# First attention layer: the values' products of a pair of heads in two shared banks, and other steps for keys, values and weights

## The reference

```python
q = q * cos + _rotate_half(q) * sin
k = k * cos + _rotate_half(k) * sin
scores = jnp.einsum('bkgqd,bksd->bkgqs', qg, k) / jnp.sqrt(...)
scores = jnp.where(causal, scores, -jnp.inf)
attn = jax.nn.softmax(scores, axis=-1)
out = jnp.einsum('bkgqs,bksd->bkgqd', attn, v)
return jnp.einsum('bso,ho->bsh', out, Wo)
```

## Time and profile before

| | |
|---|---|
| median of 3 runs | 2199.09 us (2194.62 to 2199.65) |
| profiled execution | 2196.31 us, of which the span from first to last instruction is 2194.5 us |
| the first attention layer | about 34 to 760 us of the span |
| TensorE busy | 95% of the span |
| VectorE, ScalarE, GpSimd busy | 76%, 61%, 55% |

### The profile page before, as it was taken

How to read it: one execution, slowest core, us unless ns; L and a number is a source line. 1 busy time by engine, 2 the same in 40 slices (tenths; PEclk the granted TensorE clock), 3 DMA queues, 4 the chain that set the end, 5 groups by cost and what they waited for, 6 DMA issues and landing times. The chain is left out here.

```text
span 2194.5 us, 37916 instructions
## 1 busy us (share of the span) xinstructions
PE 2089.6 (95%) x10535; PEld 1756.7 (80%) x10535; DVE 1678.1 (76%) x2972; ACT 1349.4 (61%) x3637; POOL 1216.8 (55%) x985
## 2 busy tenths in 40 slices
PE   6999999999999778999999999999999999878998
PEld 4788888888888657888888888888888888756786
DVE  6788888888888876878888788888878888875422
ACT  5877777777776455656666565666656565544321
POOL 3878777787786554546454554545445463354300
PEclk9999999999999989999999999999999999979999
DMA  2534344434344422444444444434444343533210
GB/s 83 136 100 126 108 110 113 114 105 125 104 117 130 134 62 71 116 108 116 116 109 99 121 107 115 109 100 117 114 112 112 99 116 92 131 104 105 87 53 25
DMA packets 165887, 231.69 MB, mean 106 GB/s; under 512 B 47280, under 2 KB 77136, under 8 KB 165744
## 3 DMA queue, kind: packets, MB, share of 16 engines
q1 hardware_dynamic: 165744, 229.97, 39.4%
HBM read 114.23 MB, written 6.55 MB: 55 GB/s over the span
## 5 line engine op out<-in xcount | busy, mean ns | idle before, releaser
L90 POOL TENSOR_TENSOR l_probsT_lo<-l_moved,l_probsT_hi 128x512 fp32r<-128x512 f32 (+2 forms) x256 | 278.1, 1091 | 291.9 <-ACT l_probsT_hi L946 264.5
L940 ACT ACTIVATE l_probs<-l_score,l_negtop 128x512 f32<-128x512 f32 x256 | 176.1, 688 | 354.3 <-DVE l_negtop L1051 342.3
L90 DVE TENSOR_TENSOR l_probsT_lo<-l_moved,l_probsT_hi 128x512 fp32r<-128x512 f32 (+1 forms) x256 | 285.9, 1117 | 33.4 <-ACT l_probsT_hi L946 33.4
L1831 ACT ACTIVATE l_probs<-l_score,l_negtop 128x128 f32<-128x128 f32 (+3 forms) x256 | 135.0, 527 | 170.4 <-DVE l_negtop L1944 169.6
L1051 DVE TENSOR_REDUCE l_negtop<-l_score 128x1 f32<-128x512 f32 x256 | 175.5, 686 | 74.9 <-PE l_score L85 72.6
L83 PE MATMUL l_score<-l_kT_lo,l_qT_hi 128*128 128x512 f32 (+3 forms) x512 | 190.4, 372 | 24.1 <-POOL l_qT_lo L90 9.4
L83 PE MATMUL l_out<-l_w_out_lo,l_oT_hi 128*128 128x512 f32 x512 | 209.2, 409 | 2.8 <-DVE l_oT_lo L90 2.6
L84 PE MATMUL l_out<-l_w_out_hi,l_oT_lo 128*128 128x512 f32 x512 | 201.8, 394 | 0.0
L85 PE MATMUL l_out<-l_w_out_hi,l_oT_hi 128*128 128x512 f32 x512 | 201.5, 394 | 0.0
L83 PE MATMUL l_general<-l_w_qk_lo,xT_hi 128*128 128x512 f32 x504 | 198.1, 393 | 2.5 <-PEq L1451 2.5
L1944 DVE CUSTOM_DVE_ANT_0 l_score<-l_score,l_mask 128x128 f32<-128x128 f32 (+3 forms) x256 | 126.1, 493 | 96.9 <-PE l_score L85 95.5
(11 more groups left out here) (249 smaller groups left out, 6283.4 us busy)
## 6 DMA issues: line engine op xcount, KB each, us to landing
l_moved<-l_blocks SPq DMA_DIRECT2D x1024, 64.0 KB, 2.0
l_moved<-l_blocks SPq DMA_DIRECT2D x512, 80.0 KB, 2.1
l_inv_all<-inv_rows SPq DMA_DIRECT2D x32, 512.0 KB, 4.2
l_raw_out<-l_wo SPq DMA_DIRECT2D x64, 256.0 KB, 4.2
l_inv_all<-inv_rows SPq DMA_DIRECT2D x64, 256.0 KB, 3.6
l_raw_q<-l_wq SPq DMA_DIRECT2D x32, 256.0 KB, 4.1
l_raw_qk<-l_wq SPq DMA_DIRECT2D x64, 128.0 KB, 2.9
l_raw_qk<-l_wk SPq DMA_DIRECT2D x64, 128.0 KB, 3.0
```

What stands on the lines that cost most here:

```text
L90: return engine.tensor_tensor(out, full, hi.bitcast(F32), ALU.subtract)
L940: act.activation(probs[:, n % NPR], score[n % 2][:], ACT.Exp, bias=negtop[:, n:n + 1], accum_out=total[:, n:n + 1]).then_inc(s_exp, 1)
L1831: act.activation(probs[:, n % NPR, 0:width[t]], score[n % 2][:, 0:width[t]], ACT.Exp, bias=negtop[:, n:n + 1], scale=-1.0, accum_out=total ...
```

## The change

Values' products. The two slots of a pair share their banks by tokens, no longer one bank per head. The even slot of a pair now stands for tokens of tiles 0 and 1 of both heads (2 products: 512 columns for key chunk 0, 256 for chunk 1), the odd one for tiles 2 and 3 of both heads (4 products: 512, 256, 512, 512 columns for chunks 0, 3, 1, 2). The columns multiplied are the same, 2560 a pair, in 6 products instead of 8. The odd one stands a step later (4s + 22) and is cut in two halves. `cells` gives each transposed block its place, so that a product reads runs of equal cells, and `out_item` sets which head and tile a projection step takes.

Landing. `probsT` is landed by pair in 5 pieces of 512 instead of 8 pieces of 512, 384, 256 and 128, and all of it at steps 18 to 20 of the pair, where it stood at 16, 17, 20 and 21. VectorE still makes three pieces, GpSimd two.

Other steps. Keys stand at 16b - 10 (before -14), values at 16b + 14 (before 10), their transposition at 16b + 17 (before 14); the weights' steps are set one by one. The reading of `scaled` and `oT` for the odd slot follows its `pv`. `move` waits for TensorE's `pv` before the 16 DMAs, and for VectorE's reading of `inv_all` only before the one that overwrites it.

```diff
-MOVE0_AT, LAND0_AT, PV0_AT, OUT0_AT = 8, 16, 21, 26
-USES0 = {("q", s): 4 * s - 8 for s in range(SLOTS)} | {("pv", s): 4 * s + PV0_AT for s in range(SLOTS)}
-USES0 |= {(kind, b): 16 * b + n for kind, n in (("k", -14), ("v", 10), ("vt", 14)) for b in range(B)}
+MOVE0_AT, PV0_AT, OUT0_AT = 8, 21, 26
+LAND0_AT = {18: (0, 1), 19: (2, 3), 20: (4,)}
+PIECES0, EVEN0, ODD0 = 5, (0, 1, 4), (2, 3)
+USES0 = {("q", s): 4 * s - 8 for s in range(SLOTS)} | {("pv", s): 4 * s + PV0_AT + s % 2 for s in range(SLOTS)}
+USES0 |= {(kind, b): 16 * b + n for kind, n in (("k", -10), ("v", 14), ("vt", 17)) for b in range(B)}
...
-LOADS0 = {("wq", h): 4 * h - 13 for h in range(GH)} | {("wo", h): 4 * h + 22 for h in range(GH)}
-LOADS0 |= {("wk", 0): -19, ("wv", 0): 0}
+LOADS0 = {("wq", h): n for h, n in enumerate((-17, -12, -4, 0))} | {("wo", h): n for h, n in enumerate((23, 25, 31, 33))}
+LOADS0 |= {("wk", 0): -20, ("wv", 0): 4}
...
+        PV = ([(0, slice(12, 19, 2), slice(0, 4)), (1, slice(17, 20, 2), slice(2, 4))],
+              [(0, slice(0, 4), slice(0, 4)), (3, slice(13, 16, 2), slice(1, 4, 2)), (1, slice(4, 8), slice(0, 4)),
+               (2, slice(8, 12), slice(0, 4))])
+        def out_item(slot, n):
+            return (n % 2, n // 2, n % 2 * 2 + n // 2) if slot % 2 == 0 else (2 + n % 2, n // 2, n)
...
-            for lag, pieces in ((LAND0_AT, (0, 1)), (LAND0_AT + 1, (2, 3))):
+            for lag, pieces in LAND0_AT.items():
                 slot = m.slot_at(n, lag)
-                if slot is not None:
+                if slot is not None and slot % 2 == 0:
                     for e in pieces:
-                        yield slot, e
+                        yield slot // 2, e
...
-                    for k in range(TB):
-                        right = Split(chunk_columns(probsT_hi, slot, k),
-                                      chunk_columns(probsT_lo[:, slot // 2 % 2], slot, k))
-                        last = product(nc, by_block(bank[:])[:, :, k * 32:P].rearrange("p g (t i) -> p g t i", i=32),
-                                       v[:, j // GH, k * HD:(k + 1) * HD], right, k == 0, k == TB - 1)
+                    for k, at, to in [PV[1][c] for c in part] if odd else PV[0]:
+                        right = Split(probsT_hi[:, :, at], probsT_lo[:, pair % 2, :, at])
+                        last = product(nc, bank[:].rearrange("p (g e i) -> p g e i", g=TB, e=TB)[:, :, to],
+                                       v[:, j // GH, k * HD:(k + 1) * HD], right, k == 0, k == (1, 2)[odd])
...
             def halves(x):
-                return x[0] in ("q", "k", "v")
+                return x[0] in ("q", "k", "v") or x[0] == "pv" and x[1] % 2
...
-                    slot = m.slot_at(n, PV0_AT + 3)
-                    if slot is not None:
-                        output_lo(m, slot)
+                    for odd in range(2):
+                        slot = m.slot_at(n - odd, PV0_AT + 3)
+                        if slot is not None and slot % 2 == odd:
+                            output_lo(m, slot)
```

More of the change, by code:

```diff
@@ L1610, in move @@
                     was = 2 * pair - 3
-                    sp.wait_ge(s_free, m.done(USES0, ("pv", was % SLOTS), was // SLOTS, of_dve))
+                    sp.wait_ge(s_bank, m.done(USES0, ("pv", was % SLOTS), was // SLOTS))
                     sp.nop(nofuse=True)
@@ L1617, in move @@
                 wait_past(sp, s_inv_dma, m, 32 * (SLOTS // 2), 32 * pair + 16)
+                if not (m.first and pair < 2):
+                    sp.nop(nofuse=True)
+                    sp.wait_ge(s_free, m.done(USES0, ("pv", was % SLOTS), was // SLOTS, of_dve))
                 sp.dma_start(inv_all[:, k], inv_rows[k].rearrange("p t -> (p t)").unsqueeze(0).to_broadcast([P, P * PAIR]))\
@@ L1668, in bank_use @@
                 if kind == "pv":
-                    if m.last and d == 0 and j == SLOTS - 1:
+                    if m.last and d == 0 and j == SLOTS - 1 and 0 in part:
                         linear.brief_taken(pe)
@@ L1749, in body @@
                         project(m, x, d)
-                    for x, d in m.turns(USES0, n + 1) if n + 1 < TILES else []:
+                    for x, d in m.turns(USES0, n + 1) if n + 1 < TILES or m.last else []:
                         if halves(x):
@@ L1831, in exponentials, with landed_hi @@
                 act.activation(probs[:, n % NPR, 0:width[t]], score[n % 2][:, 0:width[t]], ACT.Exp,
-                               bias=negtop[:, n:n + 1], scale=-1.0, accum_out=total[:, n:n + 1]).then_inc(s_exp, 1)
-            def landed_hi(m, slot, e):
-                pair = slot // 2
-                if slot % 2 == 0 and e == 0:
+                               bias=negtop[:, n:n + 1], scale=-1.0, accum_out=total[:, column(n):column(n) + 1]).then_inc(s_exp, 1)
+            def landed_hi(m, pair, e, n):
+                if e == 0 and n >= TILES or e == 2:
+                    if not (m.first and pair == 0):
+                        was = 2 * pair - 1
+                        act.wait_ge(s_bank, m.done(USES0, ("pv", was % SLOTS), was // SLOTS))
+                        act.nop(nofuse=True)
+                if e == 0:
                     wait_past(act, s_move[pair % 2], m, SLOTS // 4 * MOVES, (pair // 2 + 1) * MOVES)
-                act.activation(chunk_row(probsT_hi, slot, e), chunk_row(moved[:, pair % 2], slot, e), ACT.Copy)\
-                    .then_inc(s_land_hi, 1)
+                act.activation(piece(probsT_hi, e), piece(moved[:, pair % 2], e), ACT.Copy).then_inc(s_land_hi, 1)
             def output_hi(m, x, d):
@@ L1866, in body @@
                             output_hi(m, x, d)
-                    for slot, e in landing(m, n):
-                        landed_hi(m, slot, e)
+                    for pair, e in landing(m, n):
+                        landed_hi(m, pair, e, n)
                     for x, d in m.turns(USES0, n, 5):
@@ L1961, in turn_blocks, with landed_lo @@
                 rows = blocks[:, pair % 2]
-                to = rows[:, :, 0:t + 1, t + 1] if slot % 2 == 0 else rows[:, :, t, 0:t + 1]
-                dve.transpose(to.rearrange("p c k i -> p k c i"), probs[:, n % NPR, 0:width[t]]).then_inc(s_block, 1)
-            def landed_lo(m, slot, e):
-                wait_past(dve, s_land_hi, m, TILES, TB * slot + e + 1)
-                k = slot // 2 % 2
-                rest(dve, chunk_row(probsT_lo[:, k], slot, e), chunk_row(moved[:, k], slot, e),
-                     chunk_row(probsT_hi, slot, e)).then_inc(s_lo_even, 1)
+                dve.transpose(rows[:, :, cells(slot, t)].rearrange("p c k i -> p k c i"), probs[:, n % NPR, 0:width[t]]).then_inc(s_block, 1)
+            def landed_lo(m, pair, e):
+                wait_past(dve, s_land_hi, m, PIECES0 * SLOTS // 2, PIECES0 * pair + e + 1)
+                k = pair % 2
+                rest(dve, piece(probsT_lo[:, k], e), piece(moved[:, k], e), piece(probsT_hi, e)).then_inc(s_lo_even, 1)
             def output_lo(m, slot):
@@ L2007, in body @@
                             rope_cos(x, m, d)
-                    for slot, e in landing(m, n - 1):
-                        if e % 2 == 0:
-                            landed_lo(m, slot, e)
+                    for pair, e in landing(m, n - 1):
+                        if e in EVEN0:
+                            landed_lo(m, pair, e)
                     for x, d in m.turns(OUTS0, n):
-                        if x[0] % GH == GH - 1:
-                            add_rows(m, x, d)
+                        add_rows(m, x, d)
                     if m.last:
@@ L2038, in rope_lo, with landed_lo @@
                 rest(pool, to.lo, rope[:, rope_at(m, x, d)[0], 0], to.hi).then_inc(s_rope_lo, 1)
[L2040 to L2044 removed]
+            def landed_lo(m, pair, e):
+                wait_past(pool, s_land_hi, m, PIECES0 * SLOTS // 2, PIECES0 * pair + e + 1)
+                k = pair % 2
+                rest(pool, piece(probsT_lo[:, k], e), piece(moved[:, k], e), piece(probsT_hi, e)).then_inc(s_lo_odd, 1)
             for t in range(TT):
@@ L2059, in body @@
                             rope_lo(x, m, d)
-                    for slot, e in landing(m, n - 1):
-                        if e % 2:
-                            landed_lo(m, slot, e)
+                    for pair, e in landing(m, n - 1):
+                        if e in ODD0:
+                            landed_lo(m, pair, e)
                     for x, d in m.turns(LOADS0, n, 1):
```

60 lines of the change are left out of this document (32 added, 28 removed).

## The result

The changed kernel takes 2231.14 us, the median of 4 runs (2229.65 to 2232.06); the kernel before took 2196.86 (4 runs, 2193.06 to 2199.65). The ratio is 1.0156, with a 95% interval of 1.0143 to 1.0168: slower by 34 us. The forecast was 2236, its range 2197 to 2270, and slower had 0.69.

The account below looks back on a forecast made before the run. TensorE was taken to bound the kernel as long as the other engines keep up. 2196.3 + 58 (new waits) - 10.2 (fewer products) - 8.8 (small waits) = 2235.3, new median put at 2236 us, range 2197 to 2270.

Parts of the forecast that it names:

- The bound: First attention layer: TensorE bounds while the others keep up; a pass of 32 steps grows from 88.3 to 93 to 94 us.
- Fewer products: TensorE's values' products: a pair takes 3.56 us instead of 3.88, saving 0.32 a pair, 10.2 us over 32 pairs.
- VectorE's row: From step 3's scores to step 4's maximum: 6.21 us instead of 3.3, one GpSimd addition (1.29) between two landed pieces.
- the instruction that gets in twice: Rival at VectorE's two landed pieces: GpSimd goes ahead of each, another 1.29 us 28 times, 36 us, 2272; chance 0.12.
- the one that never gets in: Rival at VectorE's landed pieces: no GpSimd instruction between; chain 7.88 us, wait 0.67, total 2199, no change; chance 0.14.
- ScalarE's row: From step 4's exponential over rounding, one piece, a weight and the query bank's copy to TensorE's keys: 2.56 us.
- Who waits: TensorE reaches the keys at 7.21 us, they can start at 9.17: 1.96 us wait for ScalarE's copy, 2.07 with restart.
- the prediction's own sign (another engine named): If TensorE's new wait names an engine other than ScalarE, the chain's order is wrong though its size may hold.
- How often: Keys or values behind an even values' product: four times in six looped passes, one first, three last; 28 times 2.07, 58 us.
- The small waits: TensorE's old waits for GpSimd (5.6 us) and ScalarE (1.2) go, with 20 restarts of 0.1: about 8.8 us saved.
- Start and end of the layer: First pass: copy wait replaces GpSimd's 2.72 us, counted nothing; layer's end, where `pv` waits 4.36 us: 0, give or take 3.
- The other side: Rival: TensorE never stops for the copy, only the savings of 19 us are left, 2177 to 2180, faster; chance 0.17.

Follow-up runs that it names:

- The runs with the cut: Even values' product of 256 columns cut into two of 128: 2182.66 us on the kernel with one landed piece earlier, 2187.22 with weights earlier too.

## Why the prediction was right, and where not

**The bound.** Right: the pass grew from 88.3 to 92.6 us, a little less than the 93 to 94 forecast, and TensorE, whose work got less, spends the difference waiting.

**Fewer products.** Right, slightly low. The odd `pv` of the kernel after (start, duration):

```profile
348.39 0.40 PE L83 MATMUL l_general<-l_probsT_lo,l_v_hi 128*128 128x512 f32 x1
349.09 0.28 PE L83 MATMUL l_general<-l_probsT_lo,l_v_hi 128*128 128x256 f32 x1
349.45 0.34 PE L83 MATMUL l_score<-l_kT_lo,l_qT_hi 128*128 128x384 f32 x1
349.99 0.40 PE L83 MATMUL l_general<-l_probsT_lo,l_v_hi 128*128 128x512 f32 x1
350.68 0.39 PE L83 MATMUL l_general<-l_probsT_lo,l_v_hi 128*128 128x512 f32 x1
351.38 0.40 PE L83 MATMUL l_out<-l_w_out_lo,l_oT_hi 128*128 128x512 f32 x1
```

It takes 1.06 + 1.39 = 2.45 us (2.49 forecast), the even one 1.18 less its restart of 0.11, 1.07 as forecast; with 3.88 before, 0.36 a pair, 11.5 us instead of 10.2. The runs with the cut confirm the price of 128 columns (0.78 us a pass where waits took back 0.3 of 1.04). By the Trainium skill's isolated gap ("TensorE: Matmul & The Clock Gate", section "Back-to-back issue gap") the cut would have been almost free, and it was not.

**VectorE's row.** Right: 6.05 us against 6.21, in the order forecast, with one GpSimd instruction between the pieces. The run with the pieces ahead of the cosine shows it by taking it away; of the rivals, the instruction that gets in twice and the one that never gets in both fall. (The first, at 2272, lay 2 us beyond the range of 2197 to 2270 that the prediction says takes it in.) The rule of the Trainium skill ("SBUF — State Buffer", section "Who interferes with whom"), that such instructions exclude each other whole, agrees with 2.37 against 1.24 us.

**ScalarE's row.** Right: 2.56 us forecast and measured; the run with the weights earlier shortens it by the 0.52 of one instruction.

**Who waits.** Incomplete, and by the prediction's own sign (another engine named) wrong in its order for half of the wait. I laid TensorE's arrival at the keys against the copy and took the `pv` before them as free to run. But that `pv` reads the very piece that VectorE finishes last, at 358.12. So the wait is split in two, 0.72 for the piece and 0.94 for the copy. The sum hardly changed, since the keys' start is set by the copy either way: they start 8.98 us behind the scores (9.17 forecast), TensorE could have had them at 7.21, so 1.77 and a restart, 1.88 against 2.07. The forecast entry "about 2 us, 28 to 30 times" shows as two entries of about half. The error would have counted in a cure: an edit that frees the copy alone takes 3.9 us off a pass, not the 7.6 that both waits cost.

**How often.** The copy is waited for in full 25 times, not 28: 24 in the looped passes, none in the first, and in the last one in full and one of 0.2. 25 x 1.88 = 47.0 instead of 58.

**The small waits.** Right that they go (GpSimd's from 5.6 to 0.2), but priced by idle time: 5.6 + 1.2 and 20 restarts, 8.8. By starts the same 20 waits cost 10.0 and their restarts 2.0, so 12.0 us went.

**Start and end of the layer.** Counted at nothing, and that was the largest term left out. In the first pass I let a wait for the copy take the place of GpSimd's 2.72 us. What came are two waits for VectorE's piece, and behind each the granted clock of TensorE is at the lower of its two levels, 1.2 GHz (0.50 and 0.51 in the stretches below, which read as in the earlier trace rows; the last is of the kernel before).

```profile
79.66 0.77 PE L83 MATMUL l_general<-l_probsT_lo,l_v_hi 128*128 128x512 f32 x1 [1.82 <-DVE l_probsT_lo L90]
103.21 0.76 PE L83 MATMUL l_general<-l_probsT_lo,l_v_hi 128*128 128x512 f32 x1 [2.25 <-DVE l_probsT_lo L90]
```

```profile
79.66:85.60 5.94, 5.94 (x16) 4.84 (x17) 2.77 (x7) 2.96 (x8) 5.15 (x4) 0.50 0.68 180
103.21:106.40 3.19, 3.19 (x9) 2.71 (x10) 3.19 (x8) 3.03 (x9) 3.19 (x3) 0.51 0.62 153
```

```profile
64.02:111.00 46.98, 42.56 (x213) 34.56 (x212) 37.86 (x85) 38.58 (x94) 41.93 (x34) 1.00 0.57 154
```

Work of 9.1 us at half the rate is about 4.6 us lost, about as much as the first pass grew. The waits alone do not decide it: in the kernel before the clock stayed at 1.00 behind one of 2.72 us, and in the run with the weights earlier, which has the same two waits, it was low behind the second one only (0.57 from 100 to 104 us). So this part differs from one execution to the next, and why the clock falls stays open. At the layer's end the last `pv` waits longer than the 4.36 of the earlier trace rows:

```profile
771.81 0.68 PE L83 MATMUL l_out<-l_w_out_lo,l_oT_hi 128*128 128x512 f32 x1 [2.31 <-DVE l_oT_lo L90]
781.49 0.76 PE L83 MATMUL l_general<-l_probsT_lo,l_v_hi 128*128 128x512 f32 x1 [5.77 <-DVE l_probsT_lo L90]
```

**Sum.** The profiled execution took 2230.39, 34.1 more than that of before: 47.0 for the waits of 25 pairs, less 11.5 for the products and 12.0 for the old waits, leaves 23.5. For the looped passes alone the same prices give 26, and 25.2 were measured. The 10.6 that remain are the first pass with its lower clock, the last pass and the layer's end, which no run separated. The forecast was 39: 11 too much for the new waits, 1 too little for the products, 3 too little for the old waits, and 11 too little for the layer's ends. The loop's mechanism was right; that 2236 lies within 5 us of 2231 is luck in part, since two errors of 11 us cancel.

**The other side.** No new wait was the rival that would have made the kernel faster. In the kernel with piece and weights earlier it is nearly true: 2179.1 us, within its 2177 to 2180, with one short wait for GpSimd left in a pass. So the change holds a gain of some 17 us over the kernel before (13 to 20 by the interval), which one landed piece and a weight at the wrong step turned into a loss.

## What to carry to other kernels

When work is gathered into fewer, larger steps, add up what then stands in a row on each engine between two results that the busiest engine waits for, and add one instruction of a neighbour for each turn that a shared memory path lets it take. Look for every reader of the last result in that row, not only for the one you have in mind. And price a wait by starts, not by the idle time in brackets: here 1.35 us shown were 1.88 lost; a small extra cost on the busiest engine can likewise vanish in such holes, so measure it in a kernel that has none. Compare an edit with its forecast in one pass of the loop and not in the total alone: three totals here came within 1 us of what was worked out while the passes did not.

## What the runs showed of the hardware beyond what was expected

A matmul of 128x512 that had to wait is followed 0.32 to 0.35 us later where 0.23 is usual, behind every wait of the changed kernel from 126 to 728 us, at full clock. A `TENSOR_TENSOR` of VectorE that was next in its row got in ahead of GpSimd's addition, although they start within 0.15 us of each other (355.82 and 355.97); then, by their durations of 2.37 and 1.67, the addition ran ahead of VectorE's second one. The granted clock was 0.50 behind waits of TensorE of 1.82 and 2.25 us in one execution, and 1.00 behind one of 2.72 us in another.
